# A decoder on one core: the first expert stage with a region of rows per expert and a ranking of two groups at a time

## The reference, cut to what matters

```python
h2 = rmsnorm(X, norm2_w).reshape(B * S, d)
probs = jax.nn.softmax(h2 @ router_w, axis=-1)      # 8 experts
topw, topi = jax.lax.top_k(probs, 2)
topw = jax.nn.softmax(topw, axis=-1)
shared = swiglu(h2, sh_gate, sh_up, sh_down)         # every token
# of each token's two experts: (silu(h @ gate) * (h @ up)) @ down, weighted by topw
X + shared + spec
```

## Time and profile before

| | us |
|---|---|
| median of 3 runs (3334.71 to 3337.71) | 3335.79 |
| the profiled execution | 3304.6 |
| its span | 3302.8 |

### The profile page before, as it was taken

How to read it: one execution, slowest core, us unless ns; L and a number is a source line. 1 busy time by engine, 2 the same in 40 slices (tenths; PEclk the granted TensorE clock), 3 DMA queues, 4 the chain that set the end, 5 groups by cost and what they waited for, 6 DMA issues and landing times.

```text
span 3302.8 us, 49221 instructions
## 1 busy us (share of the span) xinstructions
PE 2773.6 (84%) x16680; PEld 1893.4 (57%) x16680; DVE 1924.6 (58%) x3389; ACT 1531.6 (46%) x2627; POOL 1467.0 (44%) x1519
## 2 busy tenths in 40 slices
PE   5878788866888788878899999799788888867998
PEld 2333333323555466644788886598455555545887
DVE  3788787874788578862122223600689888862111
ACT  4555555543776476631122221344566666642222
POOL 3576666663544477627000004600345555543444
PEclk8988999988999899989999999799899999988999
DMA  9600000000003000003556653300000100005775
GB/s 325 215 1 0 0 0 0 0 0 23 15 19 132 14 2 0 1 21 112 165 191 193 197 194 113 91 1 1 1 14 31 39 31 29 21 27 175 212 211 149
DMA packets 135984, 244.92 MB, mean 74 GB/s; under 512 B 16144, under 2 KB 107792, under 8 KB 125328
## 3 DMA queue, kind: packets, MB, share of 16 engines
q1 hardware_dynamic: 115344, 208.33, 19.5%
q0 software_dynamic: 20448, 34.11, 4.2%
HBM read 154.17 MB, written 90.05 MB: 74 GB/s over the span
## 4 chain that ended last, share of the span: by engine, by line
PE 39%; POOL 13%; DVE 11%; issue 10%; ACT 4%; POOLq 1%; DMA 1%; DVEq 0%; SPq 0%; ACTq 0%
PE PS L2188 9%; PE PS L2146 4%; PE PS L1796 4%; PE PS L2435 4%; PE PS L2422 4%; PE PS L1153 3%; PE PS L1210 2%; POOL e_hs L1355 2%; POOL rows_by_expert L2077 2%; POOL c_hs L1355 2%; PE PS L1201 2%; DVE b_mx L1258 1%; DVE e_mx L1258 1%; POOL e_qs L1358 1%; POOL rows_in_place L790 1%
## 5 line engine op out<-in xcount | busy, mean ns | idle before, releaser
L512 POOL TENSOR_TENSOR u_in<-dtx,b_rep 128x512 f32<-128x512 f32 x256 | 338.7, 1343 | 209.1 <-ACT b_rep L493 191.5
L485 PE MATMUL PS<-scaled,ident 128*128 128x512 f32 x512 | 309.9, 690 | 71.6 <-DVE scaled L522 70.9
L528 DVE TENSOR_TENSOR_SCAN state<-PS,u_in 128x512 f32<-128x512 f32 x256 | 312.6, 1221 | 94.3 <-ACT PS L501 24.4
L2209 ACT ACTIVATE d_act_b<-PS 128x256 f32<-128x256 f32 (+1 forms) x188 | 78.9, 420 | 472.5 <-PE PS L2188 472.5
L2188 PE MATMUL PS<-d_unit_T,d_w 128*128 128x256 f32 x1248 | 283.7, 381 | 1.0 <-ACT d_unit_T L2198 1.0
L2221 DVE TENSOR_TENSOR d_hid<-d_act_b,PS 128x256 f32<-128x256 f32 (+1 forms) x188 | 87.5, 466 | 316.1 <-ACT d_act_b L2209 316.1
L1355 POOL TENSOR_TENSOR e_hs<-e_pr 128x512 f32<-128x512 f32 x128 | 162.6, 1271 | 229.3 <-ACT e_pr L1322 228.1
L501 ACT ACTIVATE PS<-dt,decay_rate 128x508 f32<-128x508 f32 x256 | 174.2, 685 | 187.8 <-DVE state L528 186.9
L2188 PEld LDWEIGHTS PS<-d_unit_T,d_w 128*128 128x128 f32 x1248 | 235.2, 191 | 32.0 <-issue 1.4
L2484 POOL DMA_INDIRECT out<-f_y,f_token x78 | 121.1, 1553 | 185.9 <-DVE f_token L2468 132.3
L2146 PE MATMUL PS<-d_w,d_hid 128*128 128x256 f32 x880 | 199.4, 381 | 2.4 <-DVE d_hid L2221 2.4
(11 more groups left out here) (426 smaller groups left out, 6391.3 us busy)
## 6 DMA issues: line engine op xcount, KB each, us to landing
d_w<-in_d_w SPq DMA_DIRECT2D x41, 1024.0 KB, 4.9
f_w<-in_f_w SPq DMA_DIRECT2D x39, 1024.0 KB, 5.0
rows_in_place<-blank SPq DMA_DIRECT2D x136, 272.0 KB, 4.4
d_w<-in_d_w SPq DMA_DIRECT2D x41, 512.0 KB, 3.9
f_unit_rows<-rows_in_place SPq DMA_DIRECT2D x39, 272.0 KB, 5.1
rows_by_expert<-zeros SPq DMA_DIRECT2D x39, 256.0 KB, 2.8
d_unit_rows<-rows_by_expert SPq DMA_DIRECT2D x39, 256.0 KB, 4.0
out_by_expert<-d_y_rows SPq DMA_DIRECT2D x39, 256.0 KB, 4.0
```

What stands on the lines that cost most here:

```text
L485: nc.tensor.matmul(YB[:, c], ident[:], scaled[:, (KD * n + c) % RC], start=False, stop=n == NS - 1).then_inc(m_y, 1)
L512: nc.gpsimd.tensor_tensor(u_in[:, k % RU], dtx[:, p, c], b_rep[:, n % RB], ALU.mult).then_inc(m_u, 1)
L528: nc.vector.tensor_tensor_scan(state[:, k % 2], DECAY[:, k % RD], u_in[:, k % RU], 0.0, ALU.mult, ALU.add).then_inc(m_h, 1)
```

## The change

`experts` is written anew, for this stage alone, and `feature_rows` goes.

- `rows_by_expert` has a region of 4096 rows for each expert plus 8 spare units, as `rows_in_place` has. It is blanked at the start of the kernel by 136 more DMAs, and the 39 DMAs of zeros in the second stage go, with `zeros` and its memset. A unit's output is stored over its rows (`rows_of[:, at]`), so `out_by_expert` goes.
- PE turns H in place, without `staged_rows`; ACT takes both halves and the logits out of PSUM; each group's logits are turned back two steps later. The ranking is done for two groups at a time (`PARTS` = 4): DVE chooses on 128x64 operations, PE counts ranks with nine matmuls (`rank_tensor`), DVE makes slots. Parts 0 and 1 are ranked inside the front, parts 2 and 3 inside the first shared unit (`RANK_AT`), as is the table of units (`table_vector`), which now gives the place of each unit too.
- POOL scatters out of H directly, with no staging copy and no mark, and starts as soon as part 0 has slots.
- `SHN` = 3 shared units stand before the list, 5 after it. The shared weights have their own buffer `w_sh`. Collects have their places in `COLLECT_AT`.
- SP reads the place of a unit from the table for the load of rows and for the store (`place_of`).
- All units are written out, with no `Fori`.

The diff, cut to its core:

```diff
-    rows_by_expert = nc.dram_tensor("rows_by_expert", (UNITS * UR, D), F32, kind="Internal").ap()
-    out_by_expert = nc.dram_tensor("out_by_expert", (UNITS * UR, D), F32, kind="Internal").ap()
+    rows_by_expert = nc.dram_tensor("rows_by_expert", (E * REGION + E * UR, D), F32, kind="Internal").ap()
...
-                            pool.wait_ge(emptied, 16 * BLANKS)
+                            pool.wait_ge(emptied, 32 * BLANKS)
...
+        units = [("shared", g) for g in range(SHN)] + [("list", j) for j in range(UNITS)] + [("shared", g) for g in range(SHN, NG)]
+        LAST = len(units) - 1
+        RANK_AT = {(0, 1): 2, (0, 2): 3}
+        COLLECT_AT = {(LAST - 4, 3): [0], (LAST - 3, 1): [1], (LAST - 3, 3): [2], (LAST - 2, 1): [3], (LAST - 2, 3): [4],
+                      (LAST - 1, 0): [5], (LAST - 1, 2): [6], (LAST, 0): [7]}
+        def front_tensor(pe):
+            for step_no in range(NG + 2):
+                g = step_no
+                if g < NG:
+                    for c in range(KD):
+                        after(pe, taken_T[c], g - 1)
+                        for k in range(GS):
+                            step = nc.tensor.transpose(FT(g, c)[:, k * L:k * L + L], H[:, g, k, c * 128:c * 128 + 128], ident[:])
+                        step.then_inc(in_T[c], 1)
+                g = step_no - 1
...
+                    for c in range(KD):
+                        step = nc.tensor.matmul(LB, wr_k[:, c], xT[:, c, g], start=c == 0, stop=c == KD - 1)
+                    step.then_inc(logit, 1)
+                g = step_no - 2
...
+                        step = nc.tensor.transpose(BACK(g // 2)[:, at:at + E], lT[:, g % 2, k * L:k * L + L], ident[0:E, 0:E])
+                    step.then_inc(back, 1)
+                if step_no in (5, 8):
+                    rank_tensor(pe, (5, 8).index(step_no))
+        def rank_tensor(pe, n):
...
+            pe.wait_ge(chose, n + 1)
+            after(pe, rank_in, n)
+            picks = chosen[:, n].rearrange("p k e -> p (k e)")
+            nc.tensor.matmul(RANK, before_me, picks, start=True, stop=False)
+            for d in range(1, PART):
+                nc.tensor.matmul(RANK[:, d * E:PART * E], ones[:], picks[:, 0:(PART - d) * E], start=False, stop=False)
+            nc.tensor.matmul(RANK, ones[:], run[:, n].unsqueeze(1).broadcast_to([128, PART, E]), start=False, stop=True).then_inc(ranked, 1)
+        def front_scalar(act):
+            for step_no in range(NG + 3):
...
+                        nc.scalar.activation(xT[:, c, g], FT(g, c), ACT.Copy, scale=vec[:, c:c + 1]).then_inc(taken_T[c], 1)
...
+                    nc.scalar.activation(lT[:, g % 2], LB, ACT.Copy).then_inc(lT_in, 1)
+                n, odd = divmod(step_no - 4, 2)
+                if n >= 0 and not odd:
+                    act.wait_ge(lg_in, n + 1)
+                    nc.scalar.activation(lg[:, n], lg[:, n], ACT.Exp).then_inc(exped, 1)
+                if n >= 0 and odd:
+                    exp2_scalar(act, n)
+        def place_vector(dve, link, n):
+            dve.wait_ge(ranked, n + 1)
+            V.tensor_tensor(both[:], best[:, n], by_row(RANK).unsqueeze(1).broadcast_to([128, TOP, PART, E]), ALU.mult).then_inc(rank_in, 1)
+            dve.wait_ge(rank_in, n + 1)
+            link(V.tensor_reduce(slot_f[:], both.rearrange("p j k e -> p (j k) e"), AX.X, ALU.add))
+            V.tensor_copy(slot[:, n], slot_f[:]).then_inc(slotted, 1)
...
+        def pool(pl):
...
+            for g in range(NG):
+                pl.wait_ge(slotted, g // 2 + 1)
+                for k in range(GS):
+                    for j in range(TOP):
+                        nc.gpsimd.indirect_dma_start(rows_by_expert, slot_of(g, k, j), H[:, g, k], None).then_inc(in_list, 16)
+            for p in range(2):
+                pl.wait_ge(y_out[p], 16 * ((UNITS + 1 - p) // 2))
+            for g in range(NG):
+                after(pl, combined, g - 1)
...
+        def sync(sp):
...
+            load_weights(0)
+            load_weights(1)
+            sp.wait_ge(in_list, 16 * TOP * GS * NG)
+            load_rows(0)
+            for j in range(1, UNITS):
+                load_rows(j)
+                if j > 1:
+                    load_weights(j)
+                    store(j - 2)
...
+            sp.dma_start(rows_by_expert.rearrange("(u r p) d -> p u r d", p=128, r=UR // 128)[:, u], blank[:, :, 0:D]).then_inc(emptied, 16)
...
-                with sp.Fori(0, UNITS) as u:
-                    sp.dma_start(rows_by_expert.rearrange("(u r p) d -> p u r d", p=128, r=UR // 128)[:, u], zeros[:]).then_inc(listed, 16)
```

More of the change, by code:

```diff
@@ new lines, in output_tensor @@
+        def output_tensor(pe, v):
+            kind, at = units[v]
+            if kind == "list":
+                pe.wait_ge(w_dn[at % 2], 16 * (at // 2 + 1))
+            pe.wait_ge(hidden, v * FC + FC)
+            weights = w_sh if kind == "shared" else w[:, at % 2]
+            w_down = weights[:, UPS:].rearrange("p (f d) -> p f d", f=FC)
+            for h in range(2):
+                after(pe, taken, 2 * (v - 1) + h + 1)
+                tiles = width[kind] // 2 // 128
+                for q in range(tiles):
+                    row = (h * tiles + q) * 128
+                    for f in range(FC):
+                        step = nc.tensor.matmul(DB(h, kind)[:, q], hid[:, v % 2, f, row:row + 128], w_down[:, f], start=f == 0, stop=f == FC - 1)
+                step.then_inc(down, 1)
@@ new lines, in take_rows, with scalar @@
+        def take_rows(act, j):
+            act.wait_ge(turned, j + 1)
+            for c in range(KD):
+                step = nc.scalar.activation(unit_T[:, j % 2, c], TB[:, c], ACT.Copy, scale=vec[:, c:c + 1])
+            step.then_inc(turned_in, 1)
+        def scalar(act):
+            front_scalar(act)
+            for v, (kind, at) in enumerate(units):
+                if kind == "list" and at == 0:
+                    take_rows(act, 0)
+                for f in range(FC):
+                    after(act, hidden, v * FC + f - 1)
+                    act.wait_ge(full, v * FC + f + 1)
+                    nc.scalar.activation(act_b[:, f % 2, 0:width[kind]], GB(f, kind), ACT.Silu).then_inc(silued, 1)
+                    if f == 1 and kind == "list" and at + 1 < UNITS:
+                        take_rows(act, at + 1)
+                    if (v, f) == (0, 0):
+                        exp2_scalar(act, PARTS - 1)
@@ L2176, in unit_tensor @@
-        def unit_tensor(pe, u, kind, at, p, r, before, ahead, again=None):
-            if again == 0:
-                for sems in (w_gu, w_dn):
-                    pe.wait_ge(sems[0], 16 * (UNITS // 2 + 2))
-            for f in range(FC):
-                after(pe, hidden, u * FC + (f - 1))
-                if f == 0 and kind == "list":
-                    wait_ring(pe, w_gu, at, r)
-                    pe.wait_ge(turned_in, at + 1)
-                for b, wt in ((GB(f, kind), w_gate), (UB(f, kind), w_up))[:2 if gated else 1]:
-                    for c in range(KD):
-                        x = xT_g[:, c, at] if kind == "shared" else unit_T[:, p, c]
-                        step = nc.tensor.matmul(b, wt[:, r, c, f * 128:f * 128 + 128], x, start=c == 0, stop=c == KD - 1)
-                step.then_inc(full, 1)
-                if f == 0 and before is not None:
-                    output_tensor(pe, u - 1, *before)
-                if f == 1 and ahead == "list":
-                    turn_rows(pe, at + 1, 1 - p)
@@ L2215, in unit_vector @@
-        def unit_vector(dve, u, kind, at, p, r, before, ahead, again=None):
-            for f in range(FC):
-                if gated:
-                    if f == 0:
-                        after(dve, down, 2 * u)
-                    dve.wait_ge(silued, u * FC + (f + 1))
-                    nc.vector.tensor_tensor(hid[:, p, f, 0:width[kind]], act_b[:, f % 2, 0:width[kind]], UB(f, kind), ALU.mult).then_inc(hidden, 1)
-                if f == 0 and before is not None:
-                    output_vector(dve, u - 1, *before)
-                if kind == "shared" and again is None and (f == 1 or f == 3 and ahead):
-                    stage_group(dve, u + f // 2, 1 - f // 2)
-                if again and f % 2 == 0:
-                    collect_group(dve, again - 1, f // 2)
```

723 lines of the change are left out of this document (233 added, 490 removed).

## The result

The kernel after takes 3356.07 us (median of 4, 3352.66 to 3360.39), the kernel before beside it 3336.75 (4 runs): ratio 1.0059, 95% interval 1.0044 to 1.0074. That is 19 us slower where 13 less was forecast. Its profiled execution took 3354.14 us (span 3352.4), in line with its timed runs; the profile of before, on which the forecast rests, took 3304.6.

A forecast was written before the change was run, and what follows sets the result against it. The expert stage was taken as bound by the route to POOL's first scatter, its 64 scatters, PE's list, then gathers and shared units together. Front -26.6, list 0, tail +13.4 gave -13.2: 3322.6 against 3335.8, range 3313 to 3332.

The forecast's parts named there:

- the sum: Whole kernel: -26.6 + 13.4 = -13.2 us, carried from the profile's 3304.6 to the timed median 3335.8, giving 3322.6.
- front: Expert stage up to the list: earlier scatters, list starting at 1555.7 instead of 1582.3, 26.6 us gained.
- list: 39 expert units on PE: unchanged at 425.7 us, written-out code and SP's two register loads costed at 0.
- tail: Behind the list: five shared units instead of four, beside POOL's gathers, 114.3 us, 13.4 more than now.
- the cover of some 14 under the scatter: Front: three shared units end at 1541, leaving some 14 us in which a held DVE costs nothing.
- a possible 3.6: Tail: PE restarting below full clock after holds of 0.5 and 3.1 us; 1.0 taken of at most 3.6.
- the 1.45 of my sum: Tail: 1.45 us until the last product is there, ahead of PE's last output of 6.9.
- The fifth: Rival, list: PE's written-out instructions come too slowly, +10.3 in all, 3346, chance 0.07; the last stage speaks against it.
- The first: Rival, front: some 30 scatters beside the routing slowed by DVE, 0.34 each, 10 us; 3332.6, chance 0.04.
- The second: Rival, tail: it pays for the whole fifth unit, +20.6, so -6 in all, 3329.8, chance 0.12.
- the third: Rival, tail: no hold of PE, +8.7, so -17.9 in all, 3317.9, chance 0.14.
- The fourth: Rival, front: first choice 8 us late through round trips between engines, gain only 5 us, 3330.6, chance 0.05.

The follow-up runs named there:

- experiment 4: Before and after, both unchanged, on one chip without hold-ups: before 3311.12 and 3307.64, after 3299.97, ratio 0.9978.
- experiment 5: Before, unchanged, on a chip with hold-ups: 3339.26 and 3335.34; after with a wait for landing behind each eight transfers there: 3320.80, ratio 0.9955.
- experiments 1 and 2: After with a small GpSimd addition ahead of each eight transfers: 3355.39, ratio 1.006; after with the 136 new blanks issued in the third stage: 3356.65.

## Why the prediction was wrong

**The step that failed is in the sum**: "it lies 0.9% under the median of the three timed runs, 3335.8, and none of its waits in this stage is of a kind that scales with that, so I take the difference over". The 31 us were not a scale. They were hold-ups in the very stage that is changed, absent from the profile that I read and present in the timed runs: 700.3 us for the stage where there are hold-ups, 670.1 where there are none, all other stages nearly alike. I had hold-ups at nothing in both kernels, costed the change without them and was measured with them, where after loses 54 us and before 30. By stretch of the stage, after minus before (chips of experiment 4, then the first profile of after against before in experiment 5):

| | forecast | without hold-ups | with hold-ups |
|---|---|---|---|
| front | -26.6 | -26.6 | -7.2 |
| list | 0 | -0.9 | -2.8 |
| tail | +13.4 | +16.3 | +22.6 |
| stage | -13.2 | -11.2 | +12.6 |

The medians say +19. The stage alone gives 13 to 18, since two kernels that differ from after by little have 718.2 and 717.2 us in it (experiments 1 and 2), against 700.3 of before; the rest is within what single profiles scatter. The prediction saw that its profile lay 31 us under the timed runs, and took that for nothing that bears on the change.

**The front** was right where there are no hold-ups: first scatter 26.9 us into the stage (forecast 26.9), 80.5 us from the first to the last (79.9), shared units done at 102.8 (101), the list at 115.4 (115.6). From the end of the shared units to the list it is 12.6 us, so the cover of some 14 under the scatter was there. Where there are hold-ups, their 44 us in the shared units used it up.

**The list**: 426.3 against 425.7; written-out code costs nothing there that the profile shows, and the two register loads of SP neither.

**The tail**: 117.2 against 114.3 (my terms add up to 114.2). The mechanism is right, one term is too small: PE is held for 1.06 and 3.24 us where I had 0.5 and 3.1, and the output behind the 3.24 took 10.14 instead of 7.07, 3.1 of loss where I took 1.0 of a possible 3.6. The last hold, 1.47, is the 1.45 of my sum.

```profile
2062.11 7.13 PE L1986 MATMUL PS<-d_xT,d_w_sh 128*128 128x512 f32 x16 [1.06 <-DVE d_hid L2063]
2072.49 10.14 PE L1965 MATMUL PS<-d_w_sh,d_hid 128*128 128x256 f32 x32 [3.24 <-DVE d_hid L2063]
...
2094.39 7.17 PE L1965 MATMUL PS<-d_w_sh,d_hid 128*128 128x256 f32 x32 [1.47 <-DVE d_hid L2063]
```

So the stage gained 11.2 us without hold-ups (659.0 against 670.1) where 13.2 was forecast. The medians there differ by 7.7 (4.0 to 10.3 by the interval), somewhat less; the rest was not traced.

**The rivals.** The fifth said slower, 3346, by code that does not come fast enough, and put it in the list. The sign was right. The place was not: the list is untouched, and the loss is beside GpSimd's transfers. Its counter-argument, the last stage, could only clear the list. The first, scatters slowed by DVE, falls: in experiment 4 the scatters beside the routing keep 1.27 us from start to start. The Trainium skill, "GPSIMD Engine Reference", section "Key points", says that GpSimd contends with VectorE instructions in a two-port mode or with two SBUF inputs. The trace does not agree for the routing's 128x64 operations with two inputs. Not all of the routing is of that form, as the prediction had it; it has sums and reciprocals of one input too. The second and the third, a tail that pays 20.6 or 8.7, lie on either side of the 16.3 measured without hold-ups. The fourth falls with the first scatter at 26.9.

**What stays open**: what the chips with hold-ups do differently, and whether it is the chip at all or something else that differed between the sets, since no chip came twice. PE and SP show single instructions spaced out with nothing to wait for, while DVE and ACT wait for semaphores that should be due. The DMA engines are loaded unevenly meanwhile; this is the end of the long run of scatters, in the profile of after:

```profile
1539.50:1559.50 20.00, 8.29 (x14) 2.51 (x12) 0.69 (x1) 0.00 (x0) 15.35 (x16) 0.66 0.63 221
```

Their share is 0.63 there and 0.76 from 1535 to 1555, when SP's loads of weights fall in too, but 0.26 and less from 1485 to 1525 and 0.37 and less in the tail, where engines are held up as well. And the last stage keeps PE full at 0.76. So the load of the DMA engines alone does not explain the hold-ups. All this fits instructions, or semaphore signals, that arrive late while GpSimd's transfers are issued and under way; no run measured the arrival itself, so this cause is argued, not shown. Shown is where it happens, that it is absent in other sets of runs, and that pauses of GpSimd take most of it away.

## What to carry to other kernels

When the profiled execution and the timed runs of the kernel before differ by more than they scatter, find out where before costing a change: profile it again, on the chips that are timed. On some chips the other engines were held up beside long unbroken runs of GpSimd's indirect transfers; a wait for landing behind each eight made the time of the kernel after the same on both kinds, at 1.9 us a pause. A step that seems to be mere overhead, here a copy that GpSimd waits for, may be what paces it.

## What was not expected of the hardware

- The same kernel differs by 24 to 34 us from chip to chip: before 3308 to 3311 on three chips, 3335 to 3342 on the others. The granted clock does not tell them apart: 0.937 to 0.942 in the profiles without hold-ups, 0.939 in the one with them. In the two profiles compared, 13.8 us of it lie beside the scatters and 16.5 beside the gathers.
- During a hold-up PE started one 128x512 matmul each 2.80 us, and ACT once waited 32.8 us. In the last 20 us of a run of 32 transfers (40 us) DVE was busy for 0.69 us and ACT for none. With a wait for landing behind each eight, 10 us, three shared units first lost 1 to 3 us, four lost 11.
